# Attention beside a quantised gated layer on one core: score buffers of four heads by 256 queries in place of two heads by 512

## The reference, cut to what matters

```python
xn = layernorm(x)                                        # x: (4, 2048, 256)
q, k, v = heads(xn @ Wqkv.T)                             # 16 heads of 16
dots = einsum('bhid,bhjd->bhij', q, k) * 16 ** -0.5
dots = where(causal_mask, -inf, dots)
attn = softmax(dots)
a = merge(einsum('bhij,bhjd->bhid', attn, v)) @ Wout.T + bout
g = silu(fp4_linear(xn, w_gate)) * fp4_linear(xn, w_up)  # 704 features
return x + a + fp4_linear(g, w_down)
```

## Time and profile before

| | |
|---|---|
| median of three runs | 2744.95 us (2743.07 to 2747.64) |
| span of the profiled execution, first to last instruction | 2742.3 us |
| TensorE (PE) busy | 2513.9 us, 92% |
| TensorE weight loads (PEld) | 1370.3 us, 50% |
| ScalarE (ACT) busy | 2031.9 us, 74% |
| VectorE (DVE) busy | 1935.2 us, 71% |
| GpSimd (POOL) busy | 723.5 us, 26% |
| mean granted TensorE clock | 0.985 of full speed |

### The profile page before, as it was taken

One profiled execution on the slowest core, in us unless ns is written; L12 is line 12 of the kernel. 1 busy time (PEld: TensorE's weight loads), 2 busy tenths in 40 slices (PEclk: granted clock), 3 DMA queues, 4 the chain that ended last, 5 costly groups with the idle time before them and its releaser, 6 DMA issues.

```text
span 2742.3 us, 79793 instructions
## 1 busy us (share of the span) xinstructions
PE 2513.9 (92%) x28980; PEld 1370.3 (50%) x28980; DVE 1935.2 (71%) x5533; ACT 2031.9 (74%) x3502; POOL 723.5 (26%) x550
## 2 busy tenths in 40 slices
PE   2995999999999949999999999999999999999999
PEld 1883444444444424554554555545545555454455
DVE  6895999999999936656655656655656555566655
ACT  1564999999999937777758777775777775877775
POOL 3564333334433222212112111211212111212211
PEclk9998999999999979999999999999999999999999
DMA  2685455555555332202222023033122131220200
GB/s 67 237 269 134 70 72 75 75 76 75 74 71 70 48 81 41 49 26 40 48 80 47 26 36 52 22 67 76 23 48 41 26 77 49 42 48 24 42 25 32
DMA packets 118706, 177.08 MB, mean 65 GB/s; under 512 B 25648, under 2 KB 95024, under 8 KB 117808
## 3 DMA queue, kind: packets, MB, share of 16 engines
q1 hardware_dynamic: 97392, 147.33, 28.5%
q10 hardware_dynamic: 16576, 15.73, 2.2%
q0 software_dynamic: 4352, 8.92, 1.1%
HBM read 129.37 MB, written 42.53 MB: 63 GB/s over the span
## 4 chain that ended last, share of the span: by engine, by line
PE 52%; ACT 5%; issue 4%; DMA 1%; SPq 1%; DVE 0%; ACTq 0%; POOL 0%; DVEq 0%; POOLq 0%
PE S L913 16%; PE O L931 14%; PE F L951 10%; PE F L991 5%; ACT probs L1060 5%; PE F L981 2%; PE S L1002 2%; PE S L917 2%; SPq L528 1%; DMA y<-in_L_attn_x_dram 1%; PE F L944 1%; DMA q_st<-s_shift 0%; DVE o_turned L1266 0%; ACTq L1055 0%; ACT xt_hi L1085 0%
## 5 line engine op out<-in xcount | busy, mean ns | idle before, releaser
L1060 ACT ACTIVATE probs<-S 128x1024 f32<-128x1024 f32 (+3 forms) x1280 | 1065.7, 899 | 219.4 <-PE S L913 83.9
L913 PE MATMUL S<-q_st,k_st 128*32 128x512 bf16 (+3 forms) x10240 | 671.4, 352 | 102.0 <-ACT probs L1060 56.4
L730 ACT ACTIVATE m_excess<-m_DIFF 128x512 f32<-128x512 f32 (+7 forms) x1536 | 647.1, 472 | 87.3 <-PE m_DIFF L690 42.5
L748 DVE CUSTOM_DVE_ANT_0 m_excess<-m_S,m_excess 128x512 f32<-128x512 f32 (+7 forms) x1536 | 700.5, 530 | 11.0 <-PE m_S L690 9.3
L931 PE MATMUL O<-probs,v_sb 128*32 128x512 f32 (+3 forms) x5120 | 608.7, 532 | 2.0 <-POOL v_sb L1137 2.0
L688 PE MATMUL m_S<-m_k,m_q 128*128 128x512 bf16 (+7 forms) x1536 | 482.1, 324 | 26.7 <-DVE m_row_max L748 17.4
L688 PE MATMUL m_DIFF<-m_k,m_q_diff 128*128 128x512 bf16 (+7 forms) x1536 | 476.9, 318 | 29.6 <-DMA m_q_diff<-s_q 29.3
L913 PEld LDWEIGHTS S<-q_st,k_st 128*32 128x32 bf16 x10240 | 242.6, 95 | 457.2 <-ACT probs L1060 250.8
L632 POOL TENSOR_TENSOR m_q_diff<-m_zero,m_q 48x4096 bf16<-48x4096 bf16 x32 | 224.4, 7013 | 427.8 <-DMA m_q<-s_q 417.1
L688 PEld LDWEIGHTS m_S<-m_k,m_q 128*128 128x128 bf16 x1536 | 147.9, 96 | 276.8 <-DVE m_row_max L748 196.1
L1254 DVE TENSOR_TENSOR ht_lo<-F,ht_hi 128x512 fp32r<-128x512 f32 (+1 forms) x128 | 71.1, 558 | 231.4 <-ACT ht_hi L1075 231.4
(11 more groups left out here) (163 smaller groups left out, 4149.7 us busy)
## 6 DMA issues: line engine op xcount, KB each, us to landing
k_st<-s_k SPq DMA_DIRECT2D x96, 256.0 KB, 8.6
q_st<-s_q SPq DMA_DIRECT2D x384, 64.0 KB
s_q<-a_part SPq DMA_DIRECT2D x48, 256.0 KB, 3.0
s_k<-a_part SPq DMA_DIRECT2D x48, 256.0 KB, 2.2
m_q<-s_q SPq DMA_DIRECT2D x96, 128.0 KB, 3.8
m_k<-s_k SPq DMA_DIRECT2D x96, 128.0 KB, 6.6
m_q_diff<-s_q SPq DMA_DIRECT2D x96, 128.0 KB, 8.1
m_k<-s_k SPq DMA_DIRECT2D x96, 124.0 KB, 5.2
```

What stands on the lines that cost most here:

```text
L730: act.activation(excess[u % MAX_EXCESS][:, 0:keys // 2], DIFF[u % MAX_BUFS][:, 0:keys // 2], ACT.Relu) \
L748: dve.tensor_tensor_reduce(larger, S[u % MAX_BUFS][:, 0:keys // 2], larger, 1.0, -3e38, ALU.add, ALU.max, column).then_inc(reduced[u % MAX ...
L913: ins = pe.matmul(S[half][at, s % 2, 0:st.width], k_st[p][:, s, st.j * P + at.start:st.j * P + at.stop], q_st[st.c % 2][:, s, st.skip:QC], ...
L1060: act.activation(probs[half][st.n % 2][:, :, 0:st.width], S[half][:, :, 0:st.width], ACT.Exp, scale=SCALE).then_inc(exped[half], 1)
```

## The change

A score buffer now holds all four heads of the group for 256 of the chunk's queries (`QH`). Half 0 is the first 256 queries of the chunk, half 1 the second. `QPart` gives, for a step and half, the queries that are left after the mask (`lo`, `width`), whether any are (`live`), whether the diagonal lies in it (`masked`), and its number among the live parts of that half (`at`), by which semaphores are counted and `probs` alternates. In the last two steps of a chunk half 0 is not live and has no scores, exp or values. `pv_done` becomes a pair, and TensorE's order is scores 0, values 0 of the step before, scores 1, values 1 of the step before. Masks come after all scores of their half, and only in the half where the diagonal lies. Two heads share a PSUM bank; the first sets the accumulation's start (`start=s % 2 == 0`). The gated layer, its places and all DMAs stay.

```diff
+QH = QC // 2
...
+class QPart:
+    def __init__(self, half, skip):
+        self.lo = min(QH, max(0, skip - half * QH))
+        self.width = QH - self.lo
+        self.live = self.width > 0
+        self.masked = skip // QH == half
+        self.queries = slice(half * QH + self.lo, (half + 1) * QH)
+        self.at = None
...
-        probs = [two(f"probs{h}_", [P, 2, QC]) for h in range(2)]
+        probs = [two(f"probs{h}_", [P, HG, QH]) for h in range(2)]
...
-        S = [ps(f"S{h}", [P, 2, QC]) for h in range(2)]
+        S = [ps(f"S{h}", [P, HG, QH]) for h in range(2)]
...
             def scores(b, st, half):
-                p = st.hg % 2
-                pe.wait_ge(exped[half], b * nsteps + st.n + PRIMED)
+                p, part = st.hg % 2, st.parts[half]
+                pe.wait_ge(exped[half], b * nparts[half] + part.at + PRIMED)
...
-                for s in (2 * half, 2 * half + 1):
+                masked = st.diagonal and part.masked
+                for s in range(HG):
                     for at in quarters():
-                        ins = pe.matmul(S[half][at, s % 2, 0:st.width], k_st[p][:, s, st.j * P + at.start:st.j * P + at.stop],
-                                        q_st[st.c % 2][:, s, st.skip:QC], start=True, stop=not st.diagonal)
-                    if st.diagonal:
+                        ins = pe.matmul(S[half][at, s, 0:part.width], k_st[p][:, s, st.j * P + at.start:st.j * P + at.stop],
+                                        q_st[st.c % 2][:, s, part.queries], start=s % 2 == 0, stop=not masked,
+                                        skip_group_check=True)
+                if masked:
+                    for s in range(HG):
                         for at in quarters():
-                            ins = pe.matmul(S[half][at, s % 2, 0:at.stop], ident_bf[:, at], future[:, 0:at.stop],
-                                            start=False, stop=True)
+                            ins = pe.matmul(S[half][at, s, 0:at.stop], ident_bf[:, at], future[:, 0:at.stop],
+                                            start=False, stop=True, skip_group_check=True)
                 ins.then_inc(scored[half], 1)
-            def values(b, st):
-                for half in range(2):
-                    pe.wait_ge(exped[half], b * nsteps + st.n + 1 + PRIMED)
+            def values(b, st, half):
+                part = st.parts[half]
+                pe.wait_ge(exped[half], b * nparts[half] + part.at + 1 + PRIMED)
...
                 for s in range(HG):
-                    ins = pe.matmul(o[s * SLOT:(s + 1) * SLOT, st.skip:QC], v_sb[st.hg % 2][:, st.j, s * SLOT:(s + 1) * SLOT],
-                                    probs[s // 2][st.n % 2][:, s % 2, 0:st.width], start=st.first, stop=st.last)
-                ins.then_inc(pv_done, 1)
+                    ins = pe.matmul(o[s * SLOT:(s + 1) * SLOT, part.queries], v_sb[st.hg % 2][:, st.j, s * SLOT:(s + 1) * SLOT],
+                                    probs[half][part.at % 2][:, s, 0:part.width], start=st.first and half == 0,
+                                    stop=st.last or (half == 0 and half0_last[st.n]), skip_group_check=True)
+                ins.then_inc(pv_done[half], 1)
...
-                    scores(b, st, 0)
-                    scores(b, st, 1)
-                    if st.n:
-                        values(b, steps[st.n - 1])
+                    for half in range(2):
+                        if st.parts[half].live:
+                            scores(b, st, half)
+                        if st.n and steps[st.n - 1].parts[half].live:
+                            values(b, steps[st.n - 1], half)
...
             def exps(b, st, half):
-                act.wait_ge(scored[half], b * nsteps + st.n + 1 + PRIMED)
-                if st.n >= 2:
-                    act.wait_ge(pv_done, b * nsteps + st.n - 1 + PRIMED)
+                part = st.parts[half]
+                act.wait_ge(scored[half], b * nparts[half] + part.at + 1 + PRIMED)
+                if part.at >= 2:
+                    act.wait_ge(pv_done[half], b * nparts[half] + part.at - 1 + PRIMED)
...
-                act.activation(probs[half][st.n % 2][:, :, 0:st.width], S[half][:, :, 0:st.width], ACT.Exp,
+                act.activation(probs[half][part.at % 2][:, :, 0:part.width], S[half][:, :, 0:part.width], ACT.Exp,
                                scale=SCALE).then_inc(exped[half], 1)
```

More of the change, by code:

```diff
@@ L769, in __init__ @@
         self.chunk = hg * NQC + c
+        self.parts = [QPart(half, self.skip) for half in range(2)]
+class QPart:
[6 more added lines that the diff above has]
+        self.at = None
 def attention_steps():
@@ L777, in attention_steps @@
                 steps.append(Step(len(steps), hg, c, j))
+    for half in range(2):
+        live = [st.parts[half] for st in steps if st.parts[half].live]
+        for at, part in enumerate(live):
+            part.at = at
     return steps
@@ L799, in main_phase @@
     chunks = NHG * NQC
-    last_step = [st.n for st in steps if st.last]
+    nparts = [sum(st.parts[half].live for st in steps) for half in range(2)]
+    last_part = [st.parts[1].at for st in steps if st.last]
+    half0_last = [not steps[st.n + 1].parts[0].live for st in steps[:-1]] + [True]
     tiles = T // P
@@ L851, in main_phase @@
         scored, exped = sems("scored"), sems("exped")
-        pv_done, o_free, o_norm = sem("pv_done"), sems("o_free"), sem("o_norm")
+        pv_done, o_free, o_norm = sems("pv_done"), sems("o_free"), sem("o_norm")
         norm_ld, xn_made, y_ld, y_init = sem("norm_ld"), sem("xn_made"), sems("y_ld"), sem("y_init")
@@ L866, in spare @@
         def spare(m):
-            return S[m % SPARE // 2][:, m % 2, 0:D]
+            return S[m % SPARE // 2][:, m % 2 * 2, :]
         prime(nc, primed)
@@ L919, in scores @@
                 ins.then_inc(scored[half], 1)
-            def values(b, st):
-                for half in range(2):
-                    pe.wait_ge(exped[half], b * nsteps + st.n + 1 + PRIMED)
+            def values(b, st, half):
+                part = st.parts[half]
+                pe.wait_ge(exped[half], b * nparts[half] + part.at + 1 + PRIMED)
                 o = O[st.chunk % 2]
-                if st.c == 0 and st.first:
+                if st.c == 0 and st.first and half == 0:
                     pe.wait_ge(v_ready, b * NHG + st.hg + 1 + PRIMED)
-                if st.first:
+                if st.first and half == 0:
@@ L997, in project @@
                 if m < SPARE:
-                    pe.wait_ge(exped[m % SPARE // 2], b * nsteps + nsteps + PRIMED)
+                    pe.wait_ge(exped[m % SPARE // 2], (b + 1) * nparts[m % SPARE // 2] + PRIMED)
                 else:
@@ L1031, in _ @@
                 down(b, tiles - 2)
-                values(b, steps[-1])
+                values(b, steps[-1], 1)
                 for m in range(tiles):
@@ L1054, in exps @@
             def exps(b, st, half):
-                act.wait_ge(scored[half], b * nsteps + st.n + 1 + PRIMED)
-                if st.n >= 2:
-                    act.wait_ge(pv_done, b * nsteps + st.n - 1 + PRIMED)
-                else:
-                    act.wait_ge(pv_done, b * nsteps + PRIMED)
-                act.activation(probs[half][st.n % 2][:, :, 0:st.width], S[half][:, :, 0:st.width], ACT.Exp,
+                part = st.parts[half]
+                act.wait_ge(scored[half], b * nparts[half] + part.at + 1 + PRIMED)
+                if part.at >= 2:
+                    act.wait_ge(pv_done[half], b * nparts[half] + part.at - 1 + PRIMED)
+                else:
+                    act.wait_ge(pv_done[half], b * nparts[half] + PRIMED)
+                act.activation(probs[half][part.at % 2][:, :, 0:part.width], S[half][:, :, 0:part.width], ACT.Exp,
                                scale=SCALE).then_inc(exped[half], 1)
@@ L1080, in _ @@
                     op, ch = gated_op(n, k)
-                    exps(b, st, 0)
-                    exps(b, st, 1)
+                    for half in range(2):
+                        if st.parts[half].live:
+                            exps(b, st, half)
                     if op == "turn":
@@ L1132, in place_v @@
                 if hg >= 2:
-                    pool.wait_ge(pv_done, b * nsteps + last_step[(hg - 1) * NQC - 1] + 1 + PRIMED)
+                    pool.wait_ge(pv_done[1], b * nparts[1] + last_part[(hg - 1) * NQC - 1] + 1 + PRIMED)
                 else:
-                    pool.wait_ge(pv_done, b * nsteps + PRIMED)
+                    pool.wait_ge(pv_done[1], b * nparts[1] + PRIMED)
                 pool.sem_inc(aside, 1)
@@ L1264, in normalise @@
                     hg, c = divmod(chunk, NQC)
-                    dve.wait_ge(pv_done, b * nsteps + last_step[chunk] + 1 + PRIMED)
+                    dve.wait_ge(pv_done[1], b * nparts[1] + last_part[chunk] + 1 + PRIMED)
                     dve.transpose(o_turned[:, :], O[chunk % 2][:, :]).then_inc(o_free[chunk % 2], 1)
```

## The result

| | before | changed |
|---|---|---|
| median | 2745.73 us (2743.07 to 2747.64, 4 runs) | 2804.81 us (2801.95 to 2805.16, 3 runs) |
| span of the profiled execution | 2742.3 us | 2800.3 us |
| mean granted TensorE clock | 0.985 | 0.968 |

The ratio is 1.0212 (95% interval 1.0197 to 1.0226): 59 us slower, where 17 us faster was forecast. A fourth run of the changed kernel was disturbed (4782.96 us) and is left out of the median and the ratio.

What follows compares the result with a forecast made beforehand. TensorE was taken to bound the kernel, its idle time mostly scores waiting for exps. 52 us won, less 3 for instructions and 34.5 at chunk ends, plus 2, gave 16.5 off the 2742.3 span: 2728 us as median, range 2700 to 2750.

Steps and rivals of the forecast that it cites:

- What is late next: Part on later waits: queries' load gives 2 us back, fewer exps and their new reads cost nothing, no DMA added.
- the case for slower: Whole kernel slower: chance 14, from chunk ends costing more (11) and 60 cycles of overhead for each matmul (3).
- The schedule's sum: Whole kernel: 52 - 3 - 34.5 + 2 = 16.5 us off the span of 2742.3, so 2728 as median.
- The pair: A step without gated work and the step after it: 4.79 us in place of 5.22, 52 us in all.
- More, narrower matmuls: Scores and values, twice as many, half as wide: 0 to 0.04 us per full step, 3 us in all.
- The ends on one buffer: Last two steps of each chunk: half 1 alone, scores and exps in series, 34.5 us lost in all.
- The second end of a batch's first group: End of the second chunk there: both waits, 5.50 us in place of 4.56, a loss of 0.94.
- The batch: One batch's attention stretch, the second one shown: near 431 us in place of 435.
- The ends cost more: Rival, last two steps of the 64 chunks: half the ends lose 0.91 us once more, 2757 us; chance 11.
- Nothing: Rival: a matmul's fixed cost, hidden at 512 columns, shows at 256 and eats the gain, 2745 us; chance 16.
- The ends cost nothing: Rival: what the chunk ends lose is absorbed by later waits, 2696 us; chance 12.
- The rule of the Trainium skill: Rule against the forecast: overhead on all 12288 new matmuls, four at a time, about 77 us, hence 2805; chance 3.

Runs made afterwards that it cites:

- e5: The changed kernel with every keys' load spread, its six transfers let go one by one at later exps of the group before: 2727.71 us, ratio 0.9933.
- e7: The control: the kernel before the change, with all its keys' loads spread in the same way: 2743.85 us, ratio 0.9988.
- e6: The changed kernel with all keys' loads spread and the last two steps of each chunk alternating between the two score buffers: 2696.50 us, ratio 0.9813.
- e3: The kernel before the change, with a second copy of the keys into a DRAM scratch tensor behind each load: 2762.22 us, ratio 1.0059.
- e8: The changed kernel with the keys' loads of head groups 2 to 4 in two bursts of three transfers: 2759.02 us, ratio 1.0046.

## Why the prediction was wrong

**The step that failed** is in the last sentences of "What is late next" and in the part on narrower matmuls: "No DMA is added or moved", and "doubling them adds 0 to 0.04 per full step". The second counted what an instruction costs TensorE when it is there. The first overlooked that instructions come by DMA themselves: 94 packets are added, and they must pass where the keys' load holds every engine. It wasn't among the rivals; the case for slower was given 14 in 100, all of it for other reasons. The account now closes: e5 has the whole change without the shortage, 18 us faster than before (2727.71 against 2746.09, the before runs beside it), and the changed kernel is 77 us slower than e5. In the profiled spans the latter is 74.3 us, of which 54.7 are the gaps over 1 us (76.2 - 21.5); the other 20 is the same number as TensorE's added busy time (2530.5 - 2510.6), which fits work at the lower clock behind the gaps.

**The schedule's sum was right.** Forecast 2728, measured in e5 2727.71. That the two agree within 1 us is partly luck: single terms below are off by some 3 us, and spreading the loads by itself took 2 us off the kernel before (e7). But the terms can be held against rows:
- The pair. Forecast 4.79 us, measured 4.81 (1.75 + 3.06) against 5.22. The changed kernel, before the first gap:

```profile
1012.99 0.62 PE L934 MATMUL S<-q_st,k_st 128*32 128x256 bf16 x16
1013.44 0.60 PE L954 MATMUL O<-probs,v_sb 128*32 128x256 f32 x8
...
1015.99 0.62 PE L934 MATMUL S<-q_st,k_st 128*32 128x256 bf16 x16
...
1017.74 0.62 PE L934 MATMUL S<-q_st,k_st 128*32 128x256 bf16 x16
1018.19 0.60 PE L954 MATMUL O<-probs,v_sb 128*32 128x256 f32 x8
...
1020.80 0.62 PE L934 MATMUL S<-q_st,k_st 128*32 128x256 bf16 x16
```

- More, narrower matmuls. A full step with gated work takes 3.00 us (1012.99 to 1015.99) in place of 2.99, in which 24 more matmul records pass, and as many weight loads. A 256-column score takes 277 ns, a third of the way from 221 to 383 as forecast:

```profile
L934 PE MATMUL S<-q_st,k_st 128*32 128x256 bf16 x16384 | 652.2, 277 | 112.8 <-DMA q_st<-s_shift 38.9 <-issue 36.9 <-ACT probs L1086 35.4
```

- The ends on one buffer. Third chunk 4.97 forecast, 4.96 measured in e5; fourth chunk 5.95 and 5.93, to be read off here in e5, from 1527.23 to 1533.16, with the wait of the masked scores between (0.46, where some 0.6 was forecast):

```profile
1527.23 0.41 PE L947 MATMUL S<-q_st,k_st 128*32 128x128 bf16 x16
...
1529.84 0.62 PE L947 MATMUL S<-q_st,k_st 128*32 128x256 bf16 x16 [0.46 <-ACT probs L1099]
...
1531.80 0.41 PE L947 MATMUL S<-q_st,k_st 128*32 128x128 bf16 x16
...
1533.16 0.40 PE L947 MATMUL S<-q_st,k_st 128*32 128x256 bf16 x8
```

  The second end of a batch's first group was put at 5.50 and took 5.34. The loss in all was put at 34.5 us; e6, which takes the common buffer out of the ends, wins 31.2.
- The batch. About 431 us was forecast in place of 435; e5's second batch takes 431.00 and that of the changed kernel 450.89 at a lower clock, with the same busy ScalarE:

```profile
1451.71:1902.60 450.89, 421.27 (x8800) 312.62 (x8801) 254.45 (x536) 319.82 (x432) 82.20 (x84) 0.98 0.22 45
```
```profile
1432.09:1863.09 431.00, 416.14 (x8800) 308.87 (x8801) 254.96 (x536) 319.67 (x432) 82.36 (x84) 0.99 0.19 47
```

**The rivals.** "The ends cost more" (2757): not so, by the ends above. "Nothing": not so by e5. "The ends cost nothing" (2696) is no description of the change, but e6, where they do cost nearly nothing, runs at just that time. The rule of the Trainium skill (TensorEngine Tiling (Array Packing), Instruction Overhead) of about 60 cycles of overhead for each matmul gave, added to every matmul, the estimate of 2805. That is the measured time, and yet it is not the cause; the hit is luck. The trace does not agree with adding it: the full step is unchanged at 3.00 us, and with as many matmuls e5 runs at 2728. A right total from a wrong mechanism would have led to wider matmuls; what helps is spreading six transfers.

**What stays open.** Whether the instruction packets wait within the DMA engines or for memory wasn't tried, nor was the clock's share of the loss by itself: the 20 us of added busy time are read from two profiles. That e5's remaining 9.9 us of "issue" wait belong to the places where batches meet is read from the times of the gaps, not tested.

## What to carry to other kernels

Count instructions as traffic: a change that makes more and shorter ones on the busiest engine raises the rate at which it needs its code, and the page shows this in the row of q8. Wherever the DMA share of a stretch reaches 1.0 for longer than the distance of one or two code packets, look for gaps ended by "issue" in the middle of a run of matmuls, and for a lower granted clock behind them; the cure is to let the transfers go one by one, which here cost nothing. And when a kernel misses its forecast, sum its steps where it isn't disturbed before doubting the forecast's terms.

## What the runs showed of the hardware that was not expected

- Code packets (16384 bytes on q8) come late out of a burst of data transfers: in the changed kernel, with the engines full for up to 12 us, the next came 10.1 to 15.1 us after the last at all 15 loads. With the same loads spread (e5) no pause in the attention stages was over 10.0. (In the kernel before, a pause of 12 us by itself proves nothing: one of 12.15 from 1621.47 has idle engines.)
- With packets 5.8 to 5.9 us apart by the median, TensorE began to run dry at a pause of some 9 to 10 us and stood for 3.7 to 6.4 us at one of 12.0 to 15.7; with packets 8.6 apart, pauses of 11.9 to 19.2 us at the loads left one gap, of 0.61, and pauses up to 19.9 (e3) gaps of up to 1.1. What counts is the number of TensorE's records since the last packet began: in the changed kernel the gaps begin at 448 to 534.
- A gap of 4.7 us was followed by a granted clock of 0.54 and 0.61 over 8 us; one of 1.3 (e8) left it at 1.00.
